# Wave attention with tanh weights, one per head, and a quarter of the score copies on VectorE

## What is computed

```python
sim = jnp.einsum('bhid,bhjd->bhij', q, k) / jnp.sqrt(hd) / (jnp.abs(temperature)[0] + 0.1)
scores = jnp.zeros_like(sim)
for fi, freq in enumerate([31.0, 37.0, 41.0, 43.0, 47.0]):
    scores = scores + alpha[:, fi] * jnp.sin(TWO_PI * sim / freq + phi[:, fi])
w = jax.nn.sigmoid(scores)
w = w / (jnp.sum(w, axis=-1, keepdims=True) + 1e-10)
out = jnp.einsum('bhij,bhjd->bhid', w, v)
```

## Time and profile before

| | us |
|---|---|
| median of 3 executions | 3906.25 (3904.08 to 3914.47) |
| profiled execution | 3933.19 |
| its span, first to last instruction | 3931.4 |
| first sine to last output copy of wave attention | about 110 to 1940 |

### The profile page before, as it was taken

One profiled execution on the slowest core, in us unless ns is written; L12 is line 12 of the kernel. 1 busy time (PEld: TensorE's weight loads), 2 busy tenths in 40 slices (PEclk: granted clock), 3 DMA queues, 4 the chain that ended last, 5 costly groups with the idle time before them and its releaser, 6 DMA issues. The chain is left out here.

```text
span 3931.4 us, 70146 instructions
## 1 busy us (share of the span) xinstructions
PE 3171.9 (81%) x26580; PEld 1974.0 (50%) x26580; DVE 2951.2 (75%) x4169; ACT 2817.8 (72%) x2401; POOL 925.5 (24%) x983
## 2 busy tenths in 40 slices
PE   4788888888888898898638943798998998998890
PEld 2232233223323332233236941688888888887790
DVE  7788888888888888888565545678787878876562
ACT  3999999999999999999604313576776776774330
POOL 2010111011010101110001442544334435330336
PEclk8899999999999999999868977799999999998995
DMA  5877887788788877877521225412213113112122
GB/s 160 306 295 301 301 330 293 303 311 320 299 306 317 309 300 299 333 293 297 220 71 63 62 54 171 68 27 36 47 20 54 27 27 56 26 18 71 33 61 69
DMA packets 311330, 683.35 MB, mean 174 GB/s; under 512 B 155296, under 2 KB 228608, under 8 KB 310560
## 3 DMA queue, kind: packets, MB, share of 16 engines
q1 hardware_dynamic: 302368, 661.87, 48.6%
q0 software_dynamic: 8704, 17.84, 2.0%
HBM read 90.73 MB, written 52.10 MB: 36 GB/s over the span
## 5 line engine op out<-in xcount | busy, mean ns | idle before, releaser
L740 PE MATMUL psA<-wave,diag 128*128 128x512 f32 x2560 | 1174.2, 606 | 117.3 <-DVE score L879 75.0
L801 ACT ACTIVATE wave<-wave 128x2048 f32<-128x2048 int32 x640 | 1184.8, 1904 | 45.6 <-DMA wave<-score 41.5
L740 PEld LDWEIGHTS psA<-wave,diag 128*128 128x128 f32 x2560 | 468.4, 191 | 727.5 <-issue 594.4
L879 DVE SCALAR_TENSOR_TENSOR score<-wave,par,psA 128x1024 f32<-128x1024 f32 x256 | 316.3, 1278 | 290.2 <-PE psA L740 290.2
L678 POOL TENSOR_TENSOR diag<-ident,par 128x128 f32<-128x128 f32 x384 | 142.5, 399 | 1493.5 <-PE psA L740 1493.3
L851 DVE TENSOR_SCALAR score<-s,par 128x2048 int32<-128x2048 int32 x384 | 482.1, 1285 | 9.2 <-DMA wave<-score 6.1
L879 DVE SCALAR_TENSOR_TENSOR score<-wave,par,score 128x1024 f32<-128x1024 f32 x384 | 470.3, 1282 | 0.0
L1785 POOL COPY kb<-ks 48x1024 bf16<-48x1024 bf16 x160 | 320.9, 2005 | 567.3 <-PE psR L1845 380.6
L716 PE MATMUL psO<-score,Vg 128*9 128x512 f32 x1056 | 284.6, 689 | 105.0 <-ACT score L781 105.0
L1935 ACT ACTIVATE W<-psR 128x1024 f32<-128x1024 f32 x256 | 249.4, 1023 | 133.3 <-PE psR L1870 133.2
L1926 ACT COPY r<-psR 128x1024 f32<-128x1024 f32 x256 | 248.6, 1021 | 103.9 <-PE psR L1845 103.9
(11 more groups left out here) (262 smaller groups left out, 4798.0 us busy)
## 6 DMA issues: line engine op xcount, KB each, us to landing
wave<-score SPq DMA_DIRECT2D x384, 1023.9 KB, 6.3
wave<-s SPq DMA_DIRECT2D x128, 1023.9 KB, 5.2
ks<-kb_parts SPq DMA_DIRECT2D x56, 384.0 KB, 6.2
qs<-qb_parts SPq DMA_DIRECT2D x32, 384.0 KB, 6.2
ys<-f_ys SPq DMA_DIRECT2D x36, 256.0 KB
wave_out<-og SPq DMA_DIRECT2D x33, 256.0 KB, 8.2
o<-wave_out SPq DMA_DIRECT2D x8, 1024.0 KB, 5.3
qp<-qa_parts SPq DMA_DIRECT2D x32, 192.0 KB, 7.2
```

Of the source, the lines that this page charges most:

```text
L740: mm = pe.matmul(psA[:, kt, :], diag[:, h % 2, f, :], wave[:, h % 2, f, kt * L:(kt + 1) * L], start=(f == 0), stop=(f == PE_F - 1 or (h in ...
L801: act.activation(wave[:, h % 2, f, :], angle[:, h % 2, f, :], ACT.Sin, scale=float(TWO_PI / 2.0 ** 32)).then_inc(sine, 1)
L879: return dve.scalar_tensor_tensor(out=score[:, u * HG + h, cols], in0=wave[:, h % 2, f, cols], scalar=par[:, u, 1, h * NF + f:h * NF + f + ...
```

## The change

- The sigmoid is replaced by tanh: sigmoid(s) = 0.5 + 0.5 tanh(s/2). The scores become tanh(s/2) (`weigh`), one head after each head's five sines, for the head two before, instead of four in a row. The product with the values is then of the tanh, and the copy to `og` (`outputs`) halves it and adds half of the sum of the values over all keys.
- That sum comes from PE: four more matmuls for each group in `values`, with all 128 columns of a padded Vg as weights and one column of ones moving, into a new tile psV. DVE halves it (`halve_values`) after `add_sines` of head 2.
- Ahead of the loop ACT executes a Silu on one column, whose result nobody reads.
- For heads 0 and 2 of each group (EVAC_HEADS) DVE copies the second half of the scores, by a `tensor_scalar` from psS ahead of `add_sines` of the head two before; ACT no longer does.
- The test for the other branch becomes: a head's absolute amplitudes in sum, or the rescaled old bound, is 6 or more. In that branch the sigmoid stays, one per head.

```diff
+EVAC_HEADS = (0, 2)
+NEAR = 6.0
@@ gpsimd
+            pool.memset(Vg[:], 0.0).then_inc(pads_clear, 1)
@@ tensor, values
                     pe.wait_ge(v_ready, g + 1)
+                    pe.wait_ge(half_ready, g + C_HALF)
+                    for kt in range(QT):
+                        mm = pe.matmul(psV[:], Vg[:, slot ^ 1, kt, :, :].rearrange("p h d -> p (h d)"),
+                                       Vg[:, slot ^ 1, kt, 0, HD:VW], start=(kt == 0), stop=(kt == QT - 1))
+                    mm.then_inc(v_summed, 1)
@@ scalar
-            def sigmoids(g, slot):
-                for h in range(HG):
-                    act.wait_ge(added, g * HG * ADDS - (HG - 1 - h) * ADDS + C_ADDED)
-                    act.activation(score[:, slot * HG + h, :], score[:, slot * HG + h, :], ACT.Sigmoid)\
-                       .then_inc(weighed, 1)
+            def weigh(m, at, general):
+                act.wait_ge(added, (m + 1) * ADDS + C_ADDED)
+                if general:
+                    act.activation(score[:, at, :], score[:, at, :], ACT.Sigmoid).then_inc(weighed, 1)
+                else:
+                    act.activation(score[:, at, :], score[:, at, :], ACT.Tanh, scale=0.5).then_inc(weighed, 1)
+                    act.wait_ge(half_ready, g + 1 + C_HALF)
+                    act.activation(og[:], psO[:], ACT.Identity, bias=half_v[:, 1 - slot:2 - slot],
+                                   scale=0.5).then_inc(out_taken, 1)
@@ scalar, pair
-                                take_scores(n + 2, tu, th, tg, f // 4, general)
-                        if h == 0:
-                            sigmoids(g, 1 - u)
+                                if f == 2 or th not in EVAC_HEADS:
+                                    take_scores(n + 2, tu, th, tg, f // 4, general)
+                        weigh(n - 2, (u * HG + h - 2) % AR, general)
@@ scalar, ahead of the branches
+            act.activation(og[:, 0:1], params[:, 0, 0, 0:1], ACT.Silu)
             act.wait_ge(far_ready, 1)
@@ vector
+            def take_scores(n, u, h, ng, general):
+                cols = slice(HALF, 2 * HALF)
+                dve.wait_ge(s_ps, n * 2 + 2 + C_SPS)
+                if not (isinstance(n, int) and n < 2):
+                    dve.wait_ge(carried[0][h % 2], (ng * (HG // 2) + h // 2) * 16)
...
+                    dve.wait_ge(par_ready, ng + 1)
+                    dve.tensor_scalar(first[:, h % SR, cols], psS[:].rearrange("p a n -> p (a n)"),
+                                      float(2 ** FRAC) / FREQS[0], par[:, u, 0, h * NF:h * NF + 1],
+                                      ALU.mult, ALU.add).then_inc(s_ready, 1)
+            def halve_values(g, u):
+                dve.wait_ge(v_summed, g + 1)
+                dve.wait_ge(out_taken, g - 1 + C_TAKEN)
+                dve.tensor_scalar(half_v[:, u:u + 1], psV[:], 0.5, None, ALU.mult).then_inc(half_ready, 1)
@@ vector, pair
                             make_angles(n + 1, nu, nh, ng, general)
+                        tu, th, tg = (u, h + 2, g) if h < HG - 2 else (1 - u, h + 2 - HG, g + 1)
+                        if th in EVAC_HEADS and not (last and u == 1 and h >= HG - 2):
+                            take_scores(n + 2, tu, th, tg, general)
                         add_sines(n, u, h, g)
+                        if h == 2:
+                            halve_values(g, u)
@@ vector, the test
-            dve.tensor_scalar(far[:], bound[:], FAR * min(FREQS) / HD, None, ALU.is_ge).then_inc(far_ready, 1)
+            dve.tensor_scalar(reach[:, 0:1], bound[:], NEAR * HD / (FAR * min(FREQS)), None, ALU.mult).then_inc(reached, 1)
...
+            dve.tensor_scalar(far[:], top_reach[:], NEAR, None, ALU.is_ge).then_inc(far_ready, 1)
```

More of the change, by code:

```diff
@@ L572, in wave_attention @@
         og = sb(c, "og", [P, L])
-        Vg = sb(c, "Vg", [P, 2, QT, HG, VW])
+        Vg = sb(c, "Vg", [P, 2, QT, HG, P // HG])
+        half_v = sb(c, "half_v", [P, 2])
+        reach = sb(c, "reach", [P, 1 + H])
+        top_reach = sb(c, "top_reach", [P, 1])
         psS = ps(c, "psS", [P, 2, L])
@@ L576, in wave_attention @@
         psO = ps(c, "psO", [P, L])
+        psV = ps(c, "psV", [P, 1])
         qk_loaded = [sem(c, f"qk_loaded{i}") for i in range(2)]
@@ L598, in wave_attention @@
         far_ready = sem(c, "far_ready")
+        v_summed = sem(c, "v_summed")
+        half_ready = sem(c, "half_v_ready")
+        pads_clear = sem(c, "pads_clear")
+        reached = sem(c, "reached")
         reduced = sem(c, "reduced")
@@ L695, in _ @@
                               (used, C_USED), (summed, C_SUMMED), (added, C_ADDED), (diag_ready, C_DIAG),
-                              (out_taken, C_TAKEN),
+                              (out_taken, C_TAKEN), (half_ready, C_HALF),
+                              (weighed, C_WEIGHED),
                               (out_stored, C_STORED)):
@@ L776, in take_scores, with outputs @@
                                    scale=float(2 ** FRAC) / FREQS[0]).then_inc(s_ready, 1)
-            def sigmoids(g, slot):
-                for h in range(HG):
-                    act.wait_ge(added, g * HG * ADDS - (HG - 1 - h) * ADDS + C_ADDED)
-                    act.activation(score[:, slot * HG + h, :], score[:, slot * HG + h, :], ACT.Sigmoid)\
-                       .then_inc(weighed, 1)
-            def outputs(g):
+            def weigh(m, at, general):
[4 more added lines that the diff above has]
+                    act.activation(score[:, at, :], score[:, at, :], ACT.Tanh, scale=0.5).then_inc(weighed, 1)
+            def outputs(g, slot, general):
                 act.wait_ge(valued, 2 * g + 2 + C_VALUED)
                 act.wait_ge(out_stored, g * 16 + C_STORED)
-                act.copy(og[:], psO[:]).then_inc(out_taken, 1)
+                if general:
+                    act.copy(og[:], psO[:]).then_inc(out_taken, 1)
+                else:
+                    act.wait_ge(half_ready, g + 1 + C_HALF)
+                    act.activation(og[:], psO[:], ACT.Identity, bias=half_v[:, 1 - slot:2 - slot],
+                                   scale=0.5).then_inc(out_taken, 1)
             def pair(gg, last, general):
@@ L804, in pair @@
                                 tu, th, tg = (u, h + 2, g) if h < HG - 2 else (1 - u, h + 2 - HG, g + 1)
-                                take_scores(n + 2, tu, th, tg, f // 4, general)
-                        if h == 0:
-                            sigmoids(g, 1 - u)
+                                if f == 2 or th not in EVAC_HEADS:
+                                    take_scores(n + 2, tu, th, tg, f // 4, general)
+                        weigh(n - 2, (u * HG + h - 2) % AR, general)
                         if h == HG - 1:
-                            outputs(g)
+                            outputs(g, 1 - u, general)
             def all_heads(general):
                 for h in range(2):
-                    for half in range(2):
-                        take_scores(h, 0, h, 0, half, general)
+                    take_scores(h, 0, h, 0, 0, general)
+                    if h not in EVAC_HEADS:
+                        take_scores(h, 0, h, 0, 1, general)
                 act.wait_ge(cleared, 2)
@@ L818, in all_heads @@
                 pair(NG // 2 - 1, True, general)
-                sigmoids(NG, 1)
-                outputs(NG)
+                for h in (HG - 2, HG - 1):
+                    weigh((NG - 1) * HG + h, HG + h, general)
+                outputs(NG, 1, general)
+            act.activation(og[:, 0:1], params[:, 0, 0, 0:1], ACT.Silu)
             act.wait_ge(far_ready, 1)
@@ L852, in make_turns @@
                                   ALU.mult, ALU.add).then_inc(done, 1)
+            def take_scores(n, u, h, ng, general):
[3 more added lines that the diff above has]
+                    dve.wait_ge(carried[0][h % 2], (ng * (HG // 2) + h // 2) * 16)
+                if general:
+                    dve.tensor_copy(s[:, h % SR, cols], psS[:].rearrange("p a n -> p (a n)")).then_inc(s_ready, 1)
+                else:
+                    dve.wait_ge(par_ready, ng + 1)
+                    dve.tensor_scalar(first[:, h % SR, cols], psS[:].rearrange("p a n -> p (a n)"),
+                                      float(2 ** FRAC) / FREQS[0], par[:, u, 0, h * NF:h * NF + 1],
+                                      ALU.mult, ALU.add).then_inc(s_ready, 1)
             def make_angles(n, u, h, gn, general):
@@ L932, in all_heads @@
             def all_heads(general):
+                if 0 in EVAC_HEADS:
+                    take_scores(0, 0, 0, 0, general)
                 make_angles(0, 0, 0, 0, general)
+                if 1 in EVAC_HEADS:
+                    take_scores(1, 0, 1, 0, general)
                 with dve.Fori(0, NG // 2 - 1) as gg:
@@ L936, in all_heads @@
                 pair(NG // 2 - 1, True, general)
+                halve_values(NG, 0)
             with dve.If(dve.value_load(far[0:1, 0:1])):
```

17 lines of the change are left out of this document (12 added, 5 removed).

## The result

The changed kernel takes 3738.0 us (median of 4 executions, 3734.7 to 3742.1) against 3908.1 for the kernel before, measured beside it (4 executions): ratio 0.9564, 95% interval 0.9547 to 0.9580. That is 170 us, or 4.4%, where 114 us were forecast, and 3 us under the low end of the range. The profiled execution has a span of 3736.4 us. Of the 195 us between the two spans, 169 lie in wave attention; the other 26 lie outside the changed stage, and are about what the profiled execution of before had over its own median. So the stage alone explains the ratio.

What follows compares the result with a forecast made beforehand. The prediction took ACT to bound the kernel before, and PE and DVE exchanging psA afterwards: 14.12 + 13.04 + 12.97 + 13.04 = 53.17 us a group instead of 56.69, with the ends 114 us less, 3792; range 3741 to 3865.

Steps and rivals of the forecast that it cites:

- the parts that leave ACT: On ACT: table loads of 3.2 us a group and two score copies of 0.99 go, leaving 50.0 a group.
- the step 0 to 1: From the start of head 0's additions on DVE to head 1's: forecast to go from 19.98 to 14.12 us.
- The copies hide behind nothing: 11.90 + 1.14 = 13.04 each.: DVE's two score copies a group lengthen the steps 1 to 2 and 3 to 0, where DVE is bound, to 13.04 us.
- nothing gained in one step is carried into the next: a step costs the larger of PE's and DVE's path: PE and DVE share the single buffer psA, so the group was summed step by step to 53.17 us.
- two-step theory: Formed after the measurement, not forecast: PE and DVE compared over two steps, 25.76 + 25.09, is 50.85 us a group.
- the split by owners: Steps between heads' additions before the change: 11.90 us set by DVE, 12.97 by PE, 19.98 by ACT's batch of sigmoids.
- PE's four products, 1.15.: PE's four fp32 products ahead of head 0's values add 1.15 us to step 0 to 1, bounds 0.6 and 2.07.
- The slack is 1.4 us at least; this is the thinnest cover.: ACT's first sine of a head is ready for PE at least 1.4 us early, so ACT delays no step.
- The ends, -5.: Outside the 31 periods: first head about +1 less the first load, last group -5.8; together -5 us.
- The rival "ACT stays the bound", 3737.: ACT still sets the period at 51.4 us a group, saving 169 us, for 3737; chance 0.10.
- The separate tables.: On ACT, tanh and sine don't share a table: 8 loads a group, 60.3 to 61.7 us, 4040 in all; chance 0.10.
- two readings of the load at the loop's top: ACT's sine-table reload: either the table is taken as unknown there, making Silu useless, or a preceding square root required it.

Runs made afterwards that it cites:

- e4: Changed kernel with the tanh over only the first 1024 of each head's 2048 columns; ratio 0.9530 to the kernel before, period 50.82 us per four heads.
- e3: Changed kernel without the Silu ahead of the loop; ratio 1.0356 to the kernel before, period 61.04 us per four heads.
- e9: Kernel before with only DVE's score copies for heads 0 and 2 added, sigmoids still in a batch; ratio 0.9994 to the kernel before.
- e5: Changed kernel with GpSimd summing the four key tiles, so PE makes one fp32 product instead of four; ratio 0.9547 to the kernel before.
- e7: Changed kernel with DVE copying the second score halves of all four heads; ratio 0.9698 to the kernel before.

## Why the prediction was right or wrong

- **The direction, and the parts that leave ACT.** Right. No loads remained, tanh at 1.9, ACT at 49.6 of busy time in the group where 50.0 was summed, and the step 0 to 1 lost its sigmoids.
- **"The copies hide behind nothing: 11.90 + 1.14 = 13.04 each."** The steps are 13.10 and 13.09, and the copy's price was right within 0.06 (1.275 against 1.22). That these steps get longer is right; that the period does is wrong. This is the step that failed. It rests on "nothing gained in one step is carried into the next: a step costs the larger of PE's and DVE's path". It is carried, because PE's values don't wait for DVE: what DVE loses in one step PE is ahead in the next. The two copies were charged with 2.28 a group, and 53.17 less 2.28 is 50.89, near the 50.85 of the two-step theory (two smaller differences nearly cancel: PE's products are 0.27 cheaper, and the pair of steps 1 to 2 and 2 to 3 is DVE's, 0.21 longer than PE's). Measured were 51.39. The rows of before had it in them: the values began 0.14 after T(2), while PE's sum ends 0.76 after its release of DVE (9.52 - 8.76). So PE had its release of DVE done 0.6 before DVE came for it (11.29 against 11.90), and 12.97 was not PE's path from T but what was left of it. The true path is 24.88 for both steps, which is 12.97 + 11.90 because PE decided the two together, so the split by owners looked right.
- **PE's four products, 1.15.** 0.88 measured; 8 us of the sum in all.
- **"The slack is 1.4 us at least; this is the thinnest cover."** The right place to look, and put at nothing: PE's waits for ACT, 35 us, cost 0.54 a group over the two-step sum. The check looked at a head's first sine only. For sines PE waited 10 times (15.6 us); it waited 39 times (19.4 us) for ACT's copy of the scores, which was not in the check. This error goes against the larger one and hides part of it.
- **The ends, -5.** From the 56.80 and 51.39 of all 127 steps, the stage's steps shrank by 172 us; the forecast for them was 115. From the first sine to the last output the stage shrank by 169, so the ends were off by some microseconds only.
- **The rival "ACT stays the bound", 3737.** The number fits, the cause doesn't (e4). It is a reminder that three engines with 50 to 51 us of work each make several stories give one number. For the same reason the range failed: its low end was built as if the copies could only be cheaper, not hidden. With the copies hidden and PE's products at the low bound (0.6) the exchange alone takes 25.48 + 25.09 = 50.57 a group, and the low end would have been 3711.
- **The separate tables.** Didn't happen, and e3 shows that the mechanism was right, with a switch at 1.41 where 1.29 was reckoned. Of its two readings of the load at the loop's top the one against it was right: with the Silu ahead of the loop no such load is left.

## What to carry to other kernels

Where two engines hand one buffer back and forth, don't add up the larger path of each step. Follow the engine's work from one true wait to its next, over as many steps as lie between, and look which of its instructions don't wait for the partner at all: these let it run ahead, and the partner's extra work in the same step is then free up to that lead.

An engine at 98% with short waits need not be the only bound: take 2 us a group off it, and if its waits grow by nearly as much, it is paced by others (e9: 1.7 of 2.0).

When an activation function changes, ask which table it shares with its neighbours; here the same change was 3.6% of loss without the shared table and 4.4% of gain with it.

## What the runs showed of the hardware

- Table loads ahead of plain copies: behind the two branches of the changed kernel the eight copies of the next stage's loop (L1055) have a load each, eight in all, 10.3 us. Before, there was none. The branches now end in different functions; whether that is the reason was not tested. The loads lie in ACT's waits for PE. From the last output copy of the attention to the load that follows the loop it is 1847.57 - 1770.96 = 76.6 us, before 2014.30 - 1938.92 = 75.4.

```profile
L1055 ACT ACT_TABLE_LOAD x8 | 10.3, 1283 | 2.8 <-PEq L557 2.6
```

- PE's clock and its waits: between 111.77 and 1771.65 us the granted clock is 1.00 where it was 0.97 in the stage before. The values that took 4.98 after a wait of 3.30 ran at a granted clock of 0.71; after the change they take 3.61 throughout the lines read. All of them together took 284.6 us before and 239.4 after, 1.4 a group. The same happened in e5 and e7 to the sums after waits of 1.5 to 1.9 (granted clock 0.68 to 0.70, 5.2 to 5.4 in place of 3.70), and there it lies in the path that sets the period.
- A switch of ACT's table costs 1.41 in e3: 1.29 from the load's start to the next one's, and 0.12 by which the instruction ahead of it no longer overlaps the next.
- Four fp32 products with 128 × 128 weights and one moving column take 0.88 to the next instruction, 0.11 for each of the eight instructions; one product (e5) takes 0.20.
